# Expert gate and up products of two batches as seven block products, in two passes over the experts

## What is computed

```python
weights = _golden_weights(x, Wr, temperature)      # [b, t, 8], from sigmoid(x @ Wr / temperature)
gate = jnp.einsum('btd,edf->betf', x, Wg)          # D = 512, E = 8, F = 512
up = jnp.einsum('btd,edf->betf', x, Wu)
h = jax.nn.silu(gate) * up
e_out = jnp.einsum('betf,efd->betd', h, Wd)
out = jnp.einsum('bte,betd->btd', weights, e_out)
```

## Time and profile before

| what | value |
|---|---|
| median of 3 runs | 2971.89 us (2971.77 to 2972.51) |
| span of the profiled execution, first to last instruction | 2969.9 us |
| own time of the profiled execution | none is given beside the three; its span is 2.0 us under their median |
| PE busy | 2949.0 us, 99% |
| mean granted clock of TensorE | 0.998 of full speed |
| DVE, ACT, POOL busy | 61%, 41%, 38% |
| experts' stage | from 1891 us to the end |

### The profile page before, as it was taken

One profiled execution on the slowest core, in us unless ns is written; L12 is line 12 of the kernel. 1 busy time (PEld: TensorE's weight loads), 2 busy tenths in 40 slices (PEclk: granted clock), 3 DMA queues, 4 the chain that ended last, 5 costly groups with the idle time before them and its releaser, 6 DMA issues. The chain is left out here.

```text
span 2969.9 us, 38192 instructions
## 1 busy us (share of the span) xinstructions
PE 2949.0 (99%) x14014; PEld 2461.3 (83%) x14014; DVE 1819.7 (61%) x2571; ACT 1230.8 (41%) x2642; POOL 1143.3 (38%) x783
## 2 busy tenths in 40 slices
PE   9999999999999999999999999999999999999998
PEld 7887888888888888888888888788888888888887
DVE  6999333333699999999999999732222222222224
ACT  6555221212466666666666666622111111211112
POOL 6886322223344444444444444623222222322222
PEclk9999999999999999999999999999999999999999
DMA  3001100000222222223222222210100000010001
GB/s 133 1 22 45 43 22 22 22 22 8 92 62 66 67 61 72 61 63 77 71 69 64 61 72 79 65 64 22 43 22 22 22 22 22 22 43 22 0 1 57
DMA packets 62042, 135.39 MB, mean 46 GB/s; under 512 B 9248, under 2 KB 9632, under 8 KB 60832
## 3 DMA queue, kind: packets, MB, share of 16 engines
q1 hardware_dynamic: 61856, 132.95, 14.7%
HBM read 90.71 MB, written 8.65 MB: 33 GB/s over the span
## 5 line engine op out<-in xcount | busy, mean ns | idle before, releaser
L771 POOL TENSOR_TENSOR ffn_in_lo<-ffn_inner,ffn_in_hi 128x512 fp32r<-128x512 f32 x191 | 249.5, 1306 | 1076.7 <-ACT ffn_in_hi L767 1076.7
L767 ACT ACTIVATE ffn_in_hi<-ffn_inner 128x512 fp32r<-128x512 f32 x192 | 121.4, 632 | 538.8 <-DVE ffn_inner L791 354.9
L44 PE MATMUL S<-xT_hi,ffn_w_hi 128*128 128x512 f32 x768 | 299.3, 390 | 0.0
L46 PE MATMUL S<-xT_hi,ffn_w_lo 128*128 128x512 f32 x768 | 298.8, 389 | 0.0
L45 PE MATMUL S<-xT_lo,ffn_w_hi 128*128 128x512 f32 x768 | 298.8, 389 | 0.0
L791 DVE TENSOR_TENSOR ffn_inner<-B,ffn_gated 128x512 f32<-128x512 f32 x64 | 44.3, 692 | 293.2 <-PE B L46 283.8
L791 DVE TENSOR_TENSOR ffn_inner<-S,ffn_gated 128x512 f32<-128x512 f32 x64 | 44.3, 692 | 291.4 <-PE S L46 284.9
L1951 POOL TENSOR_TENSOR lag_rnorm<-lag_norm,minus_half 128x8 f32<-128x8 f32 x64 | 105.4, 1647 | 298.9 <-DVE lag_norm L2215 298.9
L44 PE MATMUL B<-xT_hi,lag_w_hi 128*128 128x512 f32 x512 | 206.6, 403 | 0.5 <-DVE lag_c L1997 0.5
L46 PE MATMUL B<-xT_hi,lag_w_lo 128*128 128x512 f32 x512 | 200.8, 392 | 0.0
L44 PE MATMUL A<-xT_hi,lag_w_hi 128*128 128x512 f32 x512 | 200.6, 392 | 0.0
(11 more groups left out here) (439 smaller groups left out, 8078.9 us busy)
## 6 DMA issues: line engine op xcount, KB each, us to landing
lag_raw<-in_head_weights SPq DMA_DIRECT2D x64, 256.0 KB, 4.6
lag_b_row<-lag_b_scratch SPq DMA_DIRECT2D x64, 256.0 KB, 3.3
lag_rot_q<-lag_r SPq DMA_DIRECT2D x128, 128.0 KB, 2.3
lag_rot_k<-lag_r SPq DMA_DIRECT2D x128, 128.0 KB, 2.3
ffn_raw<-in_expert_gate SPq DMA_DIRECT2D x16, 512.0 KB, 3.6
ffn_raw<-in_expert_up SPq DMA_DIRECT2D x16, 512.0 KB, 4.5
ffn_raw<-in_expert_down SPq DMA_DIRECT2D x16, 512.0 KB, 5.3
ffn_raw<-in_dense_gate SPq DMA_DIRECT2D x8, 512.0 KB, 3.6
```

What stands on the lines that cost most here:

```text
L44: pe.matmul(out, lh, rh, start=first and k == 0, stop=False)
L46: done = pe.matmul(out, ll, rh, start=False, stop=last and k == n - 1)
L767: act.activation(self.in_hi[t % 2][:, f, :], self.inner[f], ACT.Copy).then_inc(self.s_hhi, 1)
L771: pool.tensor_tensor(self.in_lo[t % 2][:, f, :], self.inner[f], f32(self.in_hi[t % 2][:, f, :]), ALU.subtract).then_inc(self.s_hlo, 1)
```

## The change

The classes `PairRows`, `Paired` and `Router` take the place of `Turn` (third use), `Gated` (second use) and `Projection` (second use). The gate and up products of one chunk (128 features) for two batches are taken as one product of 2x2 blocks: block rows up and gate, contraction in two halves of 256, block columns the two batches. It is computed in seven block products of 6 matmuls (`product`: 2 blocks of the contraction by 3) instead of eight, by Strassen's scheme in Winograd's form.

- **Sums of weights**: S1 to S4, each 128x256, made by `sums` from the raw parts A11, A12, A21, A22 (POOL for chunks 0 and 1, DVE for the others); a chunk has 7 weight blocks of 256 columns to be split, in three groups of 512, 768 and 512 columns.
- **Sums of rows**: T1, T2, T3, N4 (each 128x1024) once per pair of batches, with B11, B21, B22, split into high and low.
- **Seven products** in three banks: bank 0 takes products 1, 6, 7 and 4 on top of each other, and ACT copies it to a slot after 1, 6 and 7 (`snap`); bank 1 takes product 2; bank 2 takes 5 and then 3. DVE's `corner` adds bank and slot: 11 (gate of the first batch), 22 (up of the second), 12 (gate of the second); up of the first stays in bank 0. `silu`, `inner`, `high`, `low` follow as before.
- **Two passes**: a chunk is loaded (`load`) as two transfers of 384 and 128 KB; pair (0, 1) of batches over all 32 chunks, then pair (2, 3), so the weights are loaded and split twice. Steps q = 0 to 63; the rows of the second pair are made in steps 30 and 31, in the same places.
- **Down**: a unit (v) is two chunks and has 8 tiles for the pair, through the two banks OP0 and OP1. All 8 are issued in the even steps (step 2v + 2), between the products; odd steps have none, but for step 3. Down weights have one raw buffer and one split buffer.
- **Router**: four fp32 matmuls of 8 columns per tile, 16 per batch, from the turned rows, without padding and turns.
- Batches 0 and 1 are normed and stored in the first steps of the second pass, batches 2 and 3 at the end.

```diff
+class Paired:
...
+    BLOCK = 2 * P
+    PARTS = {1: ("A11", "B11", 0), 2: ("A12", "B21", 1), 6: ("S2", "T2", 0), 7: ("S3", "T3", 0),
+             5: ("S1", "T1", 2), 4: ("A22", "N4", 0), 3: ("S4", "B22", 2)}
+    OPENS = (1, 2, 5)
...
+    WEIGHTS = ("A11", "A12", "S1", "S2", "S3", "A22", "S4")
+    RAW = ("A21", "A11", "A12", "S1", "S2", "S3", "A22", "S4")
+    GROUPS = ((0, 2), (2, 5), (5, 7))
+    FREES = (2, 7, 3)
+    NEEDS = {1: 0, 2: 0, 6: 1, 5: 1, 7: 1, 4: 2, 3: 2}
...
+    def load_down(self, sp, v, w):
+        sp.dma_start(self.down_raw, w[v % (self.chunks // 2), :, :]).then_inc(self.s_down, 16)
+    def sums(self, eng, q):
+        eng.wait_ge(self.s_raw[q % 2], (q // 2 + 1) * 32)
+        part = lambda block: self.part(q, block)
+        eng.tensor_tensor(part("S1"), part("A21"), part("A22"), ALU.add).then_inc(self.s_sum, 1)
+        eng.tensor_tensor(part("S3"), part("A11"), part("A21"), ALU.subtract).then_inc(self.s_sum, 1)
+        eng.wait_ge(self.s_sum, 4 * q + 1)
+        eng.tensor_tensor(part("S2"), part("S1"), part("A11"), ALU.subtract).then_inc(self.s_sum, 1)
+        eng.wait_ge(self.s_sum, 4 * q + 3)
+        eng.tensor_tensor(part("S4"), part("A12"), part("S2"), ALU.subtract).then_inc(self.s_sum, 1)
...
+    def split_hi(self, act, q, n):
+        if n:
+            act.wait_ge(self.s_sum, 4 * q + 2 + n)
+        else:
+            act.wait_ge(self.s_raw[q % 2], (q // 2 + 1) * 32)
+        if q > 1:
+            act.wait_ge(self.s_p, self.at["p", self.FREES[n], q - 2])
+        out, of = self.group(q, n)
+        act.activation(self.w_hi[q % 2][:, out], self.raw[q % 2][:, of], ACT.Copy).then_inc(self.s_whi, 1)
+    def split_lo(self, pool, q, n):
+        pool.wait_ge(self.s_whi, 3 * q + n + 1)
+        out, of = self.group(q, n)
+        pool.tensor_tensor(self.w_lo[q % 2][:, out], self.raw[q % 2][:, of], f32(self.w_hi[q % 2][:, out]),
+                           ALU.subtract).then_inc(self.s_wlo, 1)
...
+    def down_split_hi(self, act, v):
+        act.wait_ge(self.s_down, 16 * v + 16)
+        if v == self.total // 2 - 1:
+            act.wait_ge(self.s_p, self.at["p", 3, self.total - 2])
+        elif v:
+            act.wait_ge(self.s_d, 2 * TPB * v)
+        act.activation(self.down_parts(v)[0], self.down_raw, ACT.Copy).then_inc(self.s_dhi, 1)
+    def down_split_lo(self, pool, v):
+        hi, lo = self.down_parts(v)
+        pool.wait_ge(self.s_dhi, v + 1)
+        pool.tensor_tensor(lo, self.down_raw, f32(hi), ALU.subtract).then_inc(self.s_dlo, 1)
+    def product(self, pe, p, q):
+        block, x, n = self.PARTS[p]
+        out, first = self.bank(n, q), p in self.OPENS
+        pe.wait_ge(self.s_wlo, 3 * q + self.NEEDS[p] + 1)
+        if q % self.chunks == 0:
+            pe.wait_ge(self.rows.s_lo, self.rows.place(q // self.chunks, x))
+        if q > 1 and p == 1:
+            pe.wait_ge(self.s_in, 2 * (q - 2) + 1)
+        elif q > 1 and p == 2:
+            pe.wait_ge(self.s_c, self.at["c", 11, q - 2])
+        elif q > 1 and p == 5:
+            pe.wait_ge(self.s_c, self.at["c", 12, q - 2])
+        elif p in (6, 7, 4):
+            pe.wait_ge(self.s_snap, self.at["snap", {6: 1, 7: 2, 4: 3}[p], q])
+        elif p == 3:
+            pe.wait_ge(self.s_c, self.at["c", 22, q])
...
+    def down(self, pe, v, n):
+        t, tt = n // TPB, n % TPB
+        if n == 0:
+            pe.wait_ge(self.s_dlo, v + 1)
+        if tt == 0:
+            pe.wait_ge(self.s_lo, 2 * (2 * v + 1) + t + 1)
+        m = v * 2 * TPB + n
+        if v < self.total // 2 - 1 or n < 2:
+            until(pe, self.s_acc, m - 1)
+        elif n > 3:
+            pe.wait_ge(self.s_acc, m - 3)
...
+        product(pe, self.down_bank(v, n), left, right).then_inc(self.s_d, 1)
...
+    def snap(self, act, n, q):
+        act.wait_ge(self.s_p, self.at["p", (1, 6, 7)[n - 1], q])
+        if q > 1:
+            act.wait_ge(*((self.s_in, 2 * (q - 2) + 2) if n == 2 else (self.s_lo, 2 * (q - 2) + (1 if n == 1 else 2))))
+        act.activation(self.slot(n, q), self.bank(0, q), ACT.Copy).then_inc(self.s_snap, 1)
+    def silu(self, act, t, q):
+        act.wait_ge(self.s_c, self.at["c", (11, 12)[t], q])
+        slot = self.slot(t + 1, q)
+        act.activation(slot, slot, ACT.Silu).then_inc(self.s_silu, 1)
+    def high(self, act, t, q):
+        act.wait_ge(self.s_in, 2 * q + t + 1)
+        if q > 2:
+            act.wait_ge(self.s_d, (q - 3) // 2 * 2 * TPB + (t + 1) * TPB)
+        act.activation(self.inner_hi[q % 3][t], self.slot((1, 3)[t], q), ACT.Copy).then_inc(self.s_hi, 1)
+    def low(self, pool, t, q):
+        pool.wait_ge(self.s_hi, 2 * q + t + 1)
+        pool.tensor_tensor(self.inner_lo[q % 3][t], self.slot((1, 3)[t], q), f32(self.inner_hi[q % 3][t]),
+                           ALU.subtract).then_inc(self.s_lo, 1)
+    def corner(self, dve, n, q):
+        bank, p, slot = {11: (1, 2, 1), 22: (2, 5, 3), 12: (2, 3, 2)}[n]
+        dve.wait_ge(self.s_p, self.at["p", p, q])
+        dve.wait_ge(self.s_snap, self.at["snap", slot, q])
+        out = self.slot(slot, q)
+        dve.tensor_tensor(out, self.bank(bank, q), out, ALU.add).then_inc(self.s_c, 1)
+    def inner(self, dve, t, q):
+        dve.wait_ge(self.s_silu, self.at["silu", t, q])
+        if t == 0:
+            dve.wait_ge(self.s_p, self.at["p", 4, q])
+            up, gate, out = self.bank(0, q), self.slot(1, q), self.slot(1, q)
+        else:
+            dve.wait_ge(self.s_c, self.at["c", 22, q])
+            up, gate, out = self.slot(3, q), self.slot(2, q), self.slot(3, q)
+        dve.tensor_tensor(out, up, gate, ALU.mult).then_inc(self.s_in, 1)
...
+    def unit(self, q):
+        return max((q - 2) // 2, 0)
+    def tiles(self, q, p):
+        if q < 3:
+            return ()
+        if q == 3:
+            after = {1: (0, 1), 2: (2, 3), 4: (4, 5), 3: (6, 7)}
+        elif q == self.total - 1:
+            return ()
+        elif q % 2:
+            return ()
+        else:
+            after = {1: (0,), 2: (1,), 4: (2,), 3: (3,), 6: (4,), 5: (5, 6, 7)}
+        return after.get(p, ())
...
@@ SP @@
-                experts.load(sp, 1, expert_w)
-                for u in range(2, EUNITS):
-                    sp.wait_ge(experts.s_wlo, (u - 1) * 3)
-                    experts.load(sp, u, expert_w)
...
+                sp.wait_ge(experts.s_wlo, 3)
+                experts.load(sp, 2, a["expert_in"])
+                sp.wait_ge(s_op, STEPS * TPB)
 ...
+                for q in range(3, last_chunk + 1):
+                    sp.wait_ge(experts.s_wlo, 3 * q - 3)
+                    experts.load(sp, q, a["expert_in"])
+                    if q > 5 and q % 2:
+                        sp.wait_ge(experts.s_dlo, (q - 5) // 2)
+                        experts.load_down(sp, (q - 5) // 2, a["expert_down"])
+                    if q in (turn_at + 12, turn_at + 14):
+                        store_batch((q - turn_at - 12) // 2)
+                for v in (last_unit - 1, last_unit):
+                    sp.wait_ge(experts.s_dlo, v)
+                    experts.load_down(sp, v, a["expert_down"])
+                store_batch(2)
...
@@ PE @@
-                for u in range(last_unit):
-                    for t in range(2 if u == 0 else 0, BATCH):
-                        if t + 1 < BATCH:
-                            if u or t > 2:
-                                experts.gate_up(pe, u, t + 1)
-                        else:
-                            experts.gate_up(pe, u + 1, 0)
-                        experts.down(pe, u, t)
...
+                rows.turn(pe, 1, [S0, O, OP0, S0], norm_2.s_row, lambda t: pe.wait_ge(*(
+                    (rows.s_copy, TPB), (s_ylo, STEPS), (s_acc, STEPS * TPB), (rows.s_copy, TPB + 1))[t]))
+                router.product(pe, 0)
+                router.product(pe, 1)
+                for p in (5, 6, 7):
+                    experts.product(pe, p, 0)
+                    experts.product(pe, p, 1)
...
+                for q in range(1, last_chunk):
+                    experts.product(pe, 1, q + 1)
+                    downs(q, 1)
+                    experts.product(pe, 2, q + 1)
+                    downs(q, 2)
+                    if q == 2:
+                        pe.wait_ge(rows.s_copy, BATCH * TPB)
+                        router.product(pe, 2)
+                        router.product(pe, 3)
+                    experts.product(pe, 4, q)
+                    downs(q, 4)
+                    experts.product(pe, 3, q)
+                    downs(q, 3)
+                    experts.product(pe, 6, q + 1)
+                    downs(q, 6)
...
+                    experts.product(pe, 5, q + 1)
+                    downs(q, 5)
+                    experts.product(pe, 7, q + 1)
...
+                experts.product(pe, 4, last_chunk)
+                downs(last_chunk, 4)
+                experts.product(pe, 3, last_chunk)
+                downs(last_chunk, 3)
+                for n in range(2 * TPB):
```

(99 more changed lines are left out.)

544 lines of the change are left out of this document (343 added, 201 removed).

## The result

The changed kernel takes 3232.51 us (median of 4 runs, 3225.76 to 3234.88); the kernel before, timed with it, 2971.83. The ratio is 1.0873, with a 95% interval of 1.0858 to 1.0888: 8.7% slower. I had said 3162, with a range up to 3215. The profiled execution of the changed kernel has a span of 3229.9 us.

A forecast was written before the change was run, and what follows sets the result against it. Bound: a pure PE matmul stream, 0.2267 us each. Span 2969.9 - 87.0 - 0.6 + 20 + 4 + 197 + 45 + 8.4 + 2.1 + 1.4 = 3160.2; the median lies 2.0 above, so 3162 us, range 3100 to 3215.

The forecast's parts named there:

- The step that decides: Odd step: down weights' load issued behind the chunk's loads, so the next step's first down tile starts at 17.92, not 10.88.
- load hidden: Rival: down weights are there when ACT asks; POOL's queue costs 2.1 per pair, no clock fall; 2975 us, chance 0.08.
- Matmuls removed: Gate and up products: 384 matmuls fewer at 0.2267 us each, 87.0 us saved.
- Load: Odd steps 5 to 59: late down weights, landing 4.9 us after issue, cost 28 x 7.04 = 197 us.
- The walk: One odd step timed from the start of product 1; the third weight group's low part ends at 9.35 us.
- Clock: After each odd step's idle the granted clock falls to half: 28 x 1.6 = 45 us, ends 0 and 90.
- Opening: Steps 0 to 4: waits of 20 us, range 5 to 35, and 4 us for clock falls.
- the router: 64 small fp32 products, 128 halves of 0.11 = 14.1 us, replace padded products and turns; net -0.6.
- Turn: Steps 30 and 31, where the second pair's rows are made: DVE's added work delays the third weight group, 8.4 us.
- step 61 and end: Step 61 has its weights, only POOL's queue is late, 2.1 us; chunk 63's inner chain and the tail give 1.4.
- Clock long at half: Rival: each of the 28 idles costs twice the 1.6 us; 3207 us, chance 0.17.

The follow-up runs named there:

- run 1: Changed kernel with the down weights' load issued one chunk load earlier, in the even steps; 3010.99 us, ratio 1.0131.
- run 12: Changed kernel with down tiles spread over two steps, odd step's splits and sums relieved, and down load issued one load earlier; 2938.67 us, ratio 0.9888.
- Run 3: Changed kernel with 24 full-width matmuls of unused result added in 29 even steps, while TensorE waits for down weights; 3181.82 us, ratio 1.0707.
- run 8: Changed kernel with half of the router's products left out, 64 small fp32 matmuls fewer; 3219.05 us.

## Why the prediction was right in kind and 70 us short

**The step that decides was named rightly.** The late issue, the first down tile behind it, 29 waits for the low part, pairs well above 29.9 and a fallen clock are all in the trace, and run 1 removes them with one moved line. The rival "load hidden" gave 2975 for what run 1 measured at 3011: its 2.1 a pair for POOL's queue is right (32.2 less 29.9 is 2.3); the opening and the end that it took over were too small.

**What failed are the sizes of three terms.** Against the profile's span (3160.2 said, 3229.9 measured):

- *Matmuls removed, 87.0.* Right: 14014 - 13678 = 336 = 384 + 48 + 32 - 128, and run 12 shows the stage at 0.2264 us a matmul.
- *Load, 28 x 7.04.* The walk up to its issue was right to 0.14 us. **The load itself was mis-sized**: 4.9 us after the first issue, from two loads behind each other in the earlier trace rows; ACT starts on it 4.6 to 6.5 after, median 5.7. Three loads were issued, and the row for three (6.15) was the nearer one; I chose by bytes. What PE waits in a pair, 6.2 + 1.38 = 7.6 by the distances of starts, was 7.04 in the sum: about 16 us in 28 pairs.
- *Clock, 28 x 1.6.* **Mis-sized too, and by more**: the matmuls between two pauses lose 2.4 in the mean, about 22 us more in all. I took it from one restart, in the earlier trace rows. Run 3 gets 2.0 of the 2.4 back by keeping PE at work; part of the rest is in the first matmuls behind a wait, which come late at 1.00 as well (0.32 instead of 0.23 us behind p7's first in run 3).
- *Opening, 20 + 4, and the router, 14.1.* Between 1890 and 2030 the changed kernel's PE is idle 27.1 us where before it was 1.7; that is 25 against my 20. The router's 128 halves took 13.7 + 10.2 = 23.9 us, not 14.1: 0.19 each, and run 8, which leaves half of them out, has 0.21. Over these 140 us the granted clock is 0.79 where it was 1.00, and the full-width matmuls take 15 us more than 0.2267 each, against my 4. Together about 26 more.
- *Turn 8.4, step 61 and end 3.5.* The pair with the turn is 48.7, 8.8 above the mean of the others. From the last issue in the row to the end it is 88.9 us, about 4 more than by my sum.

The 28 pairs are 1125.7 where my terms give 28 x 38.56 + 8.4 = 1088.1, so 38 more, which the 16 and the 22 fill. 26 + 38 + 4 is 68 of the 70; the rest is not placed. The 0.11 for a half of a router product came from eight small matmuls in the earlier trace rows; no row of mine showed 64 of them behind each other.

**The range failed because I let its terms cancel.** The upper ends of load, clock and opening were +36, +45 and +15, and I wrote that they don't all fall together. All three did come out above, by 16, 22 and 26 with the router, and the last is beyond its own end: each term was a walk that counts only the waits I could see. "Clock long at half" (3207) came nearest in number. It is half right: the clock did cost more, 2.4 a pause and not 3.2, but that is a third of what was missing.

**What stays open.** The opening was read from the trace, and only the router's part of it was tested. Why the matmuls behind one pause lose 1.5 us and behind another 3.1 wasn't looked into.
